# Attention with normalised queries on one core: sums of squares in half-height tiles, added up beforehand on VectorE

## The reference

```
q = (layernorm(x) @ Wq.T)            # 32 heads of 128
k = (ctx @ Wk.T), v = (ctx @ Wv.T)   # 8 heads of 128, each serves 4 query heads
q = q * rsqrt(mean(q * q, axis=-1) + 1e-5) * q_norm_w
k = k * rsqrt(mean(k * k, axis=-1) + 1e-5) * k_norm_w
probs = softmax(q @ k.T / sqrt(128) + mask)
x = x + tanh(g) * ((probs @ v) @ Wo.T)
```

## Time and profile before

| | |
|---|---|
| median of three runs | 1184.85 us |
| profiled execution | 1184.24 us, span 1182.1 us |
| TensorE busy | 1174.3 us, 99% of the span |
| VectorE busy | 829.1 us, 70% |
| GpSimd busy | 557.6 us, 47% |
| ScalarE busy | 425.0 us, 36% |
| granted TensorE clock | full speed |
| one step of the second layer (841.1 to 867.57) | 26.47 us |

### The profile page before, as it was taken

How to read it: one execution, slowest core, us unless ns; L and a number is a source line. 1 busy time by engine, 2 the same in 40 slices (tenths; PEclk the granted TensorE clock), 3 DMA queues, 4 the chain that set the end, 5 groups by cost and what they waited for, 6 DMA issues and landing times.

```text
span 1182.1 us, 16826 instructions
## 1 busy us (share of the span) xinstructions
PE 1174.3 (99%) x6176; PEld 946.4 (80%) x6176; DVE 829.1 (70%) x1464; ACT 425.0 (36%) x748; POOL 557.6 (47%) x385
## 2 busy tenths in 40 slices
PE   9999999999999999999999999999999999999998
PEld 8888888888788888787788888777777777777776
DVE  4656646898888888889974335766666667657795
ACT  5145151322322222232451124535443343445442
POOL 5522533766767676677463112425353443535410
PEclk9999999999999999999999999999999999999999
DMA  7944725812221221211211003121221211120201
GB/s 285 289 137 154 220 101 165 290 46 80 80 84 40 89 80 44 80 45 45 98 64 36 1 1 130 47 98 36 90 79 45 80 69 64 71 89 1 79 2 72
DMA packets 57313, 106.52 MB, mean 90 GB/s; under 512 B 3632, under 2 KB 36528, under 8 KB 51888
## 3 DMA queue, kind: packets, MB, share of 16 engines
q1 hardware_dynamic: 56736, 104.82, 25.8%
q0 software_dynamic: 384, 1.05, 0.2%
q10 hardware_dynamic: 144, 0.00, 0.0%
HBM read 78.59 MB, written 27.26 MB: 90 GB/s over the span
## 4 chain that ended last, share of the span: by engine, by line
PE 94%; DVE 4%; issue 1%; ACT 0%; POOL 0%; DVEq 0%; POOLq 0%
PE ps_q L226 14%; PE ps_b L226 13%; PE ps_q L227 13%; PE ps_q L228 13%; PE ps_b L228 13%; PE ps_b L227 13%; PE ps_s L950 5%; PE ps_b L977 4%; PE ps_q L937 1%; PE ps_s L274 1%; PE ps_q L2068 1%; PE ps_b L475 1%; PE ps_s L1763 1%; PE ps_q L525 0%; DVE x_sb L1470 0%
## 5 line engine op out<-in xcount | busy, mean ns | idle before, releaser
L226 PE MATMUL ps_q<-hT_hi,wq_hi 128*128 128x512 f32 x512 | 203.3, 397 | 0.8 <-DVE q_t L1394 0.8
L227 PE MATMUL ps_q<-hT_lo,wq_hi 128*128 128x512 f32 x512 | 199.6, 390 | 0.0
L228 PE MATMUL ps_q<-hT_hi,wq_lo 128*128 128x512 f32 x512 | 199.2, 389 | 0.0
L226 PE MATMUL ps_b<-wo_hi,o_hi 128*128 128x512 f32 x440 | 171.5, 390 | 0.0
L227 PE MATMUL ps_b<-wo_lo,o_hi 128*128 128x512 f32 x440 | 171.2, 389 | 0.0
L228 PE MATMUL ps_b<-wo_hi,o_lo 128*128 128x512 f32 x440 | 171.2, 389 | 0.0
L739 POOL TENSOR_TENSOR wq_lo<-wq_raw,wq_hi 128x512 fp32r<-128x512 f32 x64 | 90.3, 1415 | 92.0 <-ACT wq_hi L733 92.0
L1281 POOL TENSOR_TENSOR qT<-q_t 128x512 f32<-128x512 f32 x64 | 89.8, 1404 | 68.0 <-DVE q_t L1394 62.8
L1470 DVE SCALAR_TENSOR_TENSOR x_sb<-ps_b,gates,x_sb 128x512 f32<-128x512 f32 x115 | 81.7, 723 | 56.2 <-PE ps_b L228 55.8
L226 PEld LDWEIGHTS ps_q<-hT_hi,wq_hi 128*128 128x128 f32 x512 | 96.1, 188 | 25.5 <-issue 1.5
L1459 DVE TENSOR_TENSOR o_lo<-ps_b,o_hi 128x512 fp32r<-128x512 f32 x128 | 81.9, 682 | 48.0 <-ACT o_hi L1156 47.2
(11 more groups left out here) (292 smaller groups left out, 2479.2 us busy)
## 6 DMA issues: line engine op xcount, KB each, us to landing
wq_raw<-in_wq SPq DMA_DIRECT2D x16, 1024.0 KB, 4.8
wo_raw<-in_wo SPq DMA_DIRECT2D x16, 1024.0 KB, 4.9
kT<-kT_spill SPq DMA_DIRECT2D x32, 256.0 KB, 4.0
v_hi<-v_hi_spill SPq DMA_DIRECT2D x16, 512.0 KB, 3.6
v_lo<-v_lo_spill SPq DMA_DIRECT2D x16, 512.0 KB, 4.6
v_hi_spill<-vs_hi SPq DMA_DIRECT2D x12, 512.0 KB, 5.4
v_lo_spill<-vs_lo SPq DMA_DIRECT2D x12, 512.0 KB, 6.7
kw_raw<-in_wk SPq DMA_DIRECT2D x4, 1024.0 KB, 9.2
```

Source lines behind the costliest of these rows:

```text
L226: nc.tensor.matmul(dst, l_hi, r_hi, start=first, stop=False)
L227: nc.tensor.matmul(dst, l_hi, r_lo, start=False, stop=False)
L228: return nc.tensor.matmul(dst, l_lo, r_hi, start=False, stop=last)
```

## The change

It has three parts. First, for units 2 to 14 of the second layer ("folded") VectorE adds the lower 64 partitions of `q_sq` onto the upper 64 for tokens 0 to 255 of the half, and the upper onto the lower for the other 256 tokens, in place: `fold_squares(u, 0)` and `fold_squares(u, 1)`. `square_sums` then has eight matmuls of 64 rows x 32 columns with 256 columns of data, which write into both banks of `ps_q`, and `turn_sums` transposes two pieces of 256 columns. Second, `score` stands before `square_sums`, and it waits for both folds. Since both banks are taken, the projection j = 0 waits for the transpositions too, not j = 1 alone. Third, at the end of the first layer VectorE's last `add_output` of unit 12 comes behind the next unit's first rotation, and GpSimd's `att_normalise` before its second addition.

```
+        def folded(u):
+            return not (isinstance(u, int) and u in (0, 1, 2 * G - 1))
+        def fold_part(r):
+            return slice(r * D // 2, (r + 1) * D // 2), slice(r * HALF // 2, (r + 1) * HALF // 2)
...
-                elif j == 1:
-                    if not (isinstance(g, int) and u == 0):
+                else:
+                    if j < 2 and not (isinstance(g, int) and u == 0):
                         pe.wait_ge(*c("ssq_t", u))
...
             def square_sums(u, h):
+                if folded(u):
+                    halves = q_sq.rearrange("p j (t c q) -> p c t j q", t=PAIRS, c=4)
+                    for k in range(4):
+                        for r in range(2):
+                            rows, cols = fold_part(r)
+                            last = nc.tensor.matmul(sums_bank(h + r)[k * QB:(k + 1) * QB, cols], ones[rows, 0:QB],
+                                                    halves[rows, k, r * PAIRS // 2:(r + 1) * PAIRS // 2], start=True, stop=True)
+                    last.then_inc(c["ssq"], 1)
+                    return
...
             def score(u, h, g):
                 pe.wait_ge(*c("q_rot", 4 * u + 4))
+                if lay and folded(u):
+                    pe.wait_ge(*c("q_fold", 2 * u + 2))
...
+                if folded(u):
+                    early, late = fold_part(0)[1], fold_part(1)[1]
+                    nc.vector.transpose(r_t[:, early], sums_bank(h)[:, early])
+                    nc.vector.transpose(r_t[:, late], sums_bank(h + 1)[:, late]).then_inc(c["ssq_t"], 1)
...
+            def fold_squares(u, r):
+                own, tok = fold_part(r)
+                other = fold_part(1 - r)[0]
+                dve.wait_ge(*c("q_sq", 4 * u + 4))
+                nc.vector.tensor_tensor(q_sq[own, :, tok], q_sq[own, :, tok], q_sq[other, :, tok], ALU.add).then_inc(c["q_fold"], 1)
+                dve.wait_ge(*c("q_fold", 2 * u + 1 + r))
...
@@ first layer's end, GpSimd (step) @@
                     wo_low(G - 1, 3)
+                    att_normalise(pool, lay, us)
                     added(1)
-                    att_normalise(pool, lay, us)
@@ first layer's end, VectorE (step, then behind the steps) @@
-                end(3)
                 if lay == 0 and last_group(g, h):
                     maxima(2 * G - 2)
+                else:
+                    end(3)
...
                 rotate(last, 1, 0)
+                add_output(last - 3, 0, 3)
                 rotate(last, 1, 1)
```

More of the change, by code:

```diff
@@ L919, in project @@
                         pe.wait_ge(*c("q_read", n - 1))
-                elif j == 1:
-                    if not (isinstance(g, int) and u == 0):
+                else:
+                    if j < 2 and not (isinstance(g, int) and u == 0):
                         pe.wait_ge(*c("ssq_t", u))
-                elif not (isinstance(g, int) and n == 0):
-                    pe.wait_ge(*c("q_rot", n if j == 0 else n - 1))
+                    if j != 1 and not (isinstance(g, int) and n == 0):
+                        pe.wait_ge(*c("q_rot", n if j == 0 else n - 1))
                 bank = query_bank(lay, h, j)
@@ L1032, in step @@
                 if do_score and lay:
-                    if not (isinstance(g, int) and (g, h) == (1, 0)):
+                    if not folded(us) and not (isinstance(g, int) and (g, h) == (1, 0)):
                         square_sums(us, 1 - h)
                     score(us, 1 - h, g if h else g - 1)
+                    if folded(us):
+                        square_sums(us, 1 - h)
                     if do_finish and values_ahead(lay, g, h):
@@ L1074, in att_pe @@
             if lay:
+                score(last - 1, 0, G - 1)
                 square_sums(last - 1, 0)
-                score(last - 1, 0, G - 1)
             project(G - 1, 1, 0)
@@ L1405, in turn_sums @@
                 dve.wait_ge(*c("ssq", u + 1))
-                nc.vector.transpose(r_t[:, :], sums_bank(h)[:, :]).then_inc(c["ssq_t"], 1)
+                if folded(u):
[3 more added lines that the diff above has]
+                else:
+                    nc.vector.transpose(r_t[:, :], sums_bank(h)[:, :]).then_inc(c["ssq_t"], 1)
                 if isinstance(u, int) and u == 2 * G - 1:
@@ L1417, in turn_sums @@
                                                      sums_of[src * QB:(src + 1) * QB, :, 0])
+                        if not folded(u) and (k, qh) == (0, 0):
+                            last.then_inc(c["q_fold"], 2)
                 last.then_inc(c["ssq_all"], 1)
+            def fold_squares(u, r):
[4 more added lines that the diff above has]
+                dve.wait_ge(*c("q_fold", 2 * u + 1 + r))
             def scale_scores(u):
@@ L1559, in step @@
                 rotated(3)
+                if lay and do_project and folded(uq):
+                    fold_squares(uq, 0)
                 end(0)
@@ L1563, in step @@
                 end(1)
+                if lay and do_project and folded(uq):
+                    fold_squares(uq, 1)
                 end(2)
```

## The result

| | kernel before | changed kernel |
|---|---|---|
| median | 1185.41 us (10 runs) | 1188.80 us (10 runs, 1188.38 to 1189.35) |
| ratio | | 1.0029, 95% interval 1.002 to 1.0038 |
| profiled execution, span | 1184.24 us, 1182.1 us | 1188.44 us, 1186.6 us |

A forecast was written before the change was run, and what follows sets the result against it. TensorE, 99% busy, was taken as the bound. Terms +0.6 - 1.0 + 0.4 + 0.8 + 0 = +0.8 us on 1184.24 gave 1185.0 profiled, 1185.6 median; range 1179.6 to 1187.2, the forecast's own 1183.4 to 1187.2.

The forecast's parts named there:

- What bounds the kernel: TensorE, busy 99% of the span, with one wait worth counting: 0.77 us at the end of the first layer.
- Sums in small tiles: Second layer, TensorE: sums of squares with eight tiles abreast take 0.57 us instead of 1.00, 0.43 us less per folded unit.
- Rival B: Upper and lower rows take turns on TensorE, so sums stay at 1.00 us: +2.0 us, 1186.9; chance 0.06.
- The folds take turns with GpSimd: VectorE's two additions per folded unit alternate with GpSimd's instructions, whole instructions at a time, and p_lo comes later.
- Rival A: The folds are hidden in VectorE's idle time, each step keeps 0.43 us: -4.6 us, 1180.2 (or 1179.6); chance 0.26.
- the prediction's sign: Trace evidence that would confirm it: q_sq additions in h = 1 steps lasting 1.9 and 2.6 us on record.
- Rival C: VectorE's fold misses its turn between two queued GpSimd instructions: +2.5 us in six h = 1 steps, about 1200; chance 0.12.
- TensorE's restart behind p_lo: Second layer's steps: values start almost at p_lo's end, for example p_lo ends at 896.6, values start at 896.65.
- h = 1 steps: Six second-layer steps, opening odd units 3 to 13: late p_lo spends the 0.43 us and adds 0.1 each, +0.6 us.
- h = 0 steps: Five second-layer steps, even units 4 to 12: first fold hidden, values start 0.2 us earlier each, -1.0 us.
- Unit 2 and the tail: Unit 2: late p_lo delays the values, +0.4 us; tail: last projection waits for the sums' transpositions, +0.8 us.
- First layer's end: Moved addition on VectorE gains nothing, as the maxima's small instructions wait for GpSimd's p_lo: 0, at best -0.66 us.

The follow-up runs named there:

- the first experiment: The changed kernel, but the projection j = 0 of units 0, 1 and 2 doesn't wait for the transposition of the sums: 1187.14 us, ratio 1.0025.
- the edit on either engine alone: Changed kernel with only VectorE's second fold moved right behind the first: 1189.65 us; or only GpSimd's third wq_lo split moved behind its normalising: 1188.63 us.
- both together: Changed kernel with VectorE's second fold right behind the first and GpSimd's third wq_lo split behind its normalising: 1183.82 us, ratio 0.9992 to the kernel before.

## Why the prediction was wrong

**What bounds the kernel: right.** TensorE is at 99% before and after, and every difference is a wait on it or a shorter run of matmuls. One reading was too narrow: 0.77 us was called the only wait worth counting, but the waits of the kernel before also have 1.0 us for `ones` by GpSimd (the first row of the last view above, which no edit touches).

**Sums in small tiles: right.** 0.59 us (forecast 0.57). That is the time of two rounds with eight tiles abreast; the Trainium skill's "TensorE: Matmul & The Clock Gate", Part 3, said that row and column tiles compose, and this trace agrees. Rival B falls.

**The folds take turns with GpSimd: right.** Rival A wanted folds of 1.2 us; they take 1.73 and 2.48 (the prediction's sign said 1.9 and 2.6, while its working gives 1.76 for the first). Rival C wanted over 3 and a fold that misses its turn between two queued GpSimd instructions; none does, and the 2.20 of a second fold behind wq_lo is one turn as well. p_lo ends 2.94 and 2.62 us behind the scores' first matmul, and the prediction's numbers give 2.9 and 2.62. In units 4 to 13 everything up to there was right to 0.05 us.

**TensorE's restart behind p_lo: the mis-sized term.** The prediction has the values start 0.05 to 0.08 us after p_lo's end ("p_lo ends at 896.6, the values start at 896.65"), as if the matmul alone had waited. They start 0.35 us after it in five h = 1 steps and 0.20 in the h = 0 steps. In the step shown the wait for p_lo opens at 872.53, and TensorE's queue still has two register instructions behind it, at 872.64 and 872.73 (one in an h = 0 step), about 0.1 us apart. With the waits reordered it is 0.15 everywhere, which takes 1.2 us off; the rest of the term is the 0.15 that any wait for p_lo cost there. So the h = 1 steps cost +2.06 and not +0.6, the h = 0 ones gain 0.28 and not 1.0: 2.2 us of the 3.6 us by which the sum was off. Before, p_lo ended 0.88 us ahead of the values; the same instructions stood at 869.53 to 869.80, while the scores still ran, and cost nothing.

**The wait behind the scores of unit 1: the step that is missing.** "Both ps_q banks now hold sums, so the projection j = 0 waits for both transpositions" was applied to the steps and the tail, but the code has the wait from the projection of unit 1 on. At that of unit 2 the sums waited for are unit 1's, unfolded and in the other bank, and no values lie between. VectorE turns those sums only behind the last part of the step's softmax (763.62, 764.78). +1.51 us, shown by the first experiment to be that wait alone.

**Unit 2 and the tail: right.** +0.36 and +0.73 against +0.4 and +0.8; the tail's is confirmed by the kernel with unit 14 unfolded.

**First layer's end: right.** 0, in the trace and in a run of its own, by the mechanism named: the small instructions wait for GpSimd's p_lo whenever they are issued.

The two misses make 3.7 us, +1.5 and +2.2, against a total of 3.6. The measured median is 3.2 us above the forecast and not 3.6, because outside its span the changed kernel takes 1.8 us where 2.1 was assumed, and because its median lies 0.4 above its profiled execution where 0.6 was assumed. By its own terms the range's upper end is 1187.5 and not 1187.2, which doesn't reach 1188.8 either.

**Open.** Unit 3 has p_lo 2.77 us behind the scores' first matmul and not 2.94, and no run separates why. Units 2 and 13 have the short restart of 0.10 us. They stand outside the hardware loop, where the semaphore counts are constants and need no register, and in the trace the last instruction ahead of the weight load carries the wait for p_lo itself:

```profile
1084.60 1.22 DVE L800 TENSOR_TENSOR p_lo<-pT,p_hi 128x1024 fp32r<-128x1024 f32 x1 [0.57 <-ACT p_hi L1170]
1085.93 0.39 PE L996 MATMUL ps_b<-p_hi,v_hi 64*128 64x256 f32 x2 [0.51 <-issue]
```

## What to carry over

When an edit moves the end of a wait from "long over" to "decides", add what stands in the waiting engine's queue between that wait and the work: put the wait that will end last also last in the queue. When a wait's condition is widened, go through every unit of the ramp and the tail for which it now holds, not only the steady step. And where VectorE and GpSimd contend, moving an instruction from one rival exposes it to the next: draw both queues, since here the edit on either engine alone was worth nothing, and both together 4.6 us.

## What the hardware showed beyond that

- VectorE and GpSimd went in turns, instruction by instruction, when both had one ready. A fold behind the shift: 1.73 us, then wq_lo 2.28 (1.30 alone), then a second fold 2.20 (1.22 alone). The Trainium skill's "SBUF — State Buffer", Who interferes with whom, has the shared ports as an exclusive lock; these rows agree. Whether the engines alternate or the one that has waited longest goes first, these rows can't tell: both would give them.
- The one who waits starts before the other's record ends: the first fold ends 1.08 us after the shift's recorded end while it takes 1.22 alone, so it must have begun 0.14 us before that end.
- Register instructions of TensorE that pass while its matmuls still run cost nothing (869.53 to 869.80 before). Behind a wait that has just opened each costs about 0.1 us (872.64, 872.73, the matmul at 872.84). From p_lo's end to the matmul that waited for it the changed kernel has 0.10, 0.20 or 0.35 us.
